# Per-edge coefficients of a graph network: three bf16 parts added in PSUM by TensorE, or in SBUF by VectorE

## The chip, the cores and the metric

One NeuronCore of a Trainium2 chip runs the whole kernel as one program. The metric is the device time of one execution in microseconds; a kernel's time is the median of its runs. Five engines work beside one another, each with its own instruction stream: TensorE (PE in the profile, its weight loads PEld), VectorE (DVE), ScalarE (ACT), GpSimd (POOL) and SyncE (SP), which issues DMAs. They meet by semaphores alone.

## The reference

A graph with 3125 nodes, 50000 edges sorted by destination, 128 features. Two blocks, each on the layer-normalised and rectified features, each added to its input:

```
def block_0(x, src, dst, W_in, b_in, W_out, b_out):
    h = x @ W_in + b_in                       # 64 wide
    ew = deg_inv_sqrt[src] * deg_inv_sqrt[dst]
    acc = cur = h
    for _ in range(3):
        cur = segment_sum(cur[dst] * ew, src)
        acc = acc + cur
    return acc / 4 @ W_out + b_out
def block_1(x, weight, w_comp, h_bias, loop_weight, norm, src, dst, etypes):
    W_rel = einsum('rb,bio->rio', w_comp, weight)      # 64 types, 16 bases
    msg = einsum('ni,rio->nro', x, W_rel)[src, etypes] * norm
    return relu(segment_sum(msg, dst) + h_bias + x @ loop_weight)
```

What the change touches is a part of block 1 that is done early: for each edge the 16 coefficients w_comp[type of the edge, :] times the weight `norm` of the edge. The edges lie in 391 tiles of 128.

## The kernel before, in words

**Setup** (to about 52 us). Edge data is loaded and tables of tiles and windows are made. A window is 16 destination nodes, 200 in all; a pair is a tile with one of the windows that it touches, S = 590 in all, worked through in 59 turns of U = 10.

**The counting stage** (about 52 to 345 us) makes the matrix CT of edge counts between nodes. Per turn VectorE (`onehots`, line 740) makes one-hot rows: every five pairs one L751, and for each pair one L754. They lie in a ring of three half turns; L749 waits until the pairs of the half that is overwritten are counted. TensorE (`count_pairs`, line 979) multiplies them, one matmul of 400 columns a pair (L992), into six rotating PSUM banks; it waits for VectorE's rows and for free banks in four groups a turn (pairs 0-2, 3-4, 5-7, 8-9). ScalarE copies two finished windows at a time out of PSUM (L1215) and clears them (L1217), SyncE stores them into CT (L426).

**The coefficients** ride along in the first 49 turns (CT_TURNS), 8 tiles of edges a turn. GpSimd loads the types of the edges, broadcast over partitions, into one of three buffers `cbuf` (`load_types`, L518), waiting for the coefficient matmuls that read the buffer before (`reload_types`, L522). After pair 4 VectorE turns them into a one-hot by type in place (`type_rows`, L721). After pair 6 TensorE multiplies them (L1000): four matmuls, each for two tiles, with 128x128 one-hot weights and a moving operand `wc_parts`. To have f32 accuracy from bf16 matmuls, w_comp is cut into three bf16 parts that add up to it (`finish_h`, L705 to L708), and the parts stand next to one another, so that the result has 2 x 16 x 3 = 96 columns. It goes to PSUM bank 6, which has no other use in these turns. In VectorE's next turn, after pair 7, a reduce adds the three parts from PSUM into `coef_sum` in SBUF (`sum_parts`, L727), and after pair 9 a multiply by the edges' weight makes `coef_out` (`finish_coefs`, L735), one of three buffers, which GpSimd stores to HBM (`store_coefs`, L529). TensorE may write bank 6 again when the reduce has read it (L996). L736 is the multiply's source.

The loops of three turns on the engines start at aligned instruction addresses. From turn 49 on there are no coefficients, and after each turn TensorE adds the columns of two finished groups of CT for the degrees (`add_degrees`, L1017, one-column matmuls, 25 a group).

**After it**: three rounds of propagation with CT (L1067, to about 520 us), the second layer norm, and block 1, which gathers rows by `src`, forms key rows with the stored coefficients (L873, L876), and multiplies (L1135, L1115). Nothing there is changed.

## Time and profile before

| | |
|---|---|
| Median of 3 runs | 1063.05 us (1062.24 to 1063.17) |
| The profiled execution | 1060.07 us |
| its span, first to last instruction | 1058.5 us |
| Mean granted TensorE clock | 0.886 |
| Busy: TensorE / VectorE / ScalarE / GpSimd | 835.4 / 777.0 / 357.5 / 477.5 us |
| Chain that ended last, by engine | TensorE 35%, VectorE 26%, issue 15% |

The span is what the trace covers; the execution's own time adds the little that lies before and after it. Busy shares are averages over stages with different limits, so a stage is read by itself. The granted clock is TensorE's share of full speed; it has two levels, 0.5 (1.2 GHz) and 1.0 (2.4 GHz). The record of an instruction lasts longer than it holds its engine up, as the next one starts before its end.

### The profile page before, as it was taken

The numbers are of one execution on the slowest core, as the hardware profiler recorded it, in microseconds if no ns is written. First come the engines' busy times: TensorE is split into PE (matmuls) and PEld (weight loads), VectorE is DVE, ScalarE is ACT, GpSimd is POOL, SyncE is SP. The second block draws the span as 40 slices with busy tenths as digits, with TensorE's granted clock in tenths as the row PEclk, the third lists the DMA queues.
The fourth block names the chain that finished last, engine by engine and source line by source line (L and its number), as shares of the span: only waits on it lengthen the run. The fifth ranks groups of instructions, "written<-read, shape, count | busy, mean of one in ns | idle before, by whom it ended". The sixth has DMA issues, their size and how long they took to land.

```text
span 1058.5 us, 27160 instructions
## 1 busy us (share of the span) xinstructions
PE 835.4 (79%) x5567; PEld 594.8 (56%) x5571; DVE 777.0 (73%) x2436; ACT 357.5 (34%) x706; POOL 477.5 (45%) x532
## 2 busy tenths in 40 slices
PE   4667667677698699999719889988888988888676
PEld 2622222222255699999517667666665665565345
DVE  7879999999984645434617777787778788888554
ACT  0402355677777000001315444443434332221000
POOL 2022323333200000010167777777777777777773
PEclk9687886977866899999858999999999999999868
DMA  4012334455534000011591111111112112111113
GB/s 114 1 45 67 85 103 107 125 131 128 132 101 107 2 1 2 1 32 51 146 298 49 48 50 50 50 50 47 52 47 52 50 50 52 50 52 51 51 50 89
DMA packets 64847, 73.24 MB, mean 69 GB/s; under 512 B 12803, under 2 KB 53178, under 8 KB 64666
## 3 DMA queue, kind: packets, MB, share of 16 engines
q1 hardware_dynamic: 48362, 37.30, 12.7%
q0 software_dynamic: 16432, 35.29, 12.6%
q8 instruction: 26, 0.43, 0.2%
q14 instruction: 27, 0.22, 0.1%
HBM read 43.85 MB, written 8.22 MB: 49 GB/s over the span
## 4 chain that ended last, share of the span: by engine, by line
PE 35%; DVE 26%; issue 15%; DVEq 9%; DMA 7%; POOL 5%; ACT 1%; SPq 1%; POOLq 0%; ACTq 0%
PE ps L1067 14%; PE ps L1135 10%; DMA CT<-h_dram,src_col 6%; POOL CT L563 5%; DVE ohbuf L754 5%; DVE CT L873 5%; PE ps L992 4%; PE ps L1115 3%; DVE u L754 3%; DVEq L876 3%; DVE CT L876 3%; DVE ohbuf L751 3%; DVEq L122 2%; DVEq L873 2%; DVE u L751 1%
## 5 line engine op out<-in xcount | busy, mean ns | idle before, releaser
L563 POOL DMA_INDIRECT CT<-h_dram,src_col x391 | 393.9, 1007 | 125.1 <-issue 95.4
L1135 PE MATMUL ps<-CT 128*128 128x256 f32 x1180 | 316.9, 418 | 71.7 <-DVE CT L876 46.3
L1135 PEld LDWEIGHTS ps<-CT 128*128 128x128 f32 x1180 | 211.3, 198 | 171.7 <-issue 151.9
L876 DVE SCALAR_TENSOR_TENSOR CT<-iota,dlP,CT 128x256 f32<-128x256 int16 x590 | 286.8, 486 | 5.6
L873 DVE COPY CT<-CT 128x128 f32 x590 | 137.7, 233 | 139.2 <-PE ps L1135 72.6
L1276 ACT COPY CT<-ps 128x256 f32<-128x256 f32 x200 | 77.7, 388 | 328.5 <-PE ps L1135 324.6
L992 PE MATMUL ps<-ohbuf 128*128 128x400 bf16 x395 | 126.6, 422 | 48.2 <-DVE ohbuf L754 34.6
L518 POOL DMA_DIRECT2D u<-types_dram x49 | 44.0, 904 | 198.8 <-PE ps L1000 185.1
L1215 ACT CAST stage<-ps 128x800 bf16<-128x800 f32 x100 | 82.4, 824 | 123.1 <-PE ps L992 122.8
L1067 PE MATMUL ps<-u,CT 128*128 128x192 bf16 x1250 | 107.4, 248 | 6.9 <-DVEq L804 6.9
L1067 PEld LDWEIGHTS ps<-u,CT 128*128 128x128 bf16 x1250 | 104.3, 99 | 9.0 <-DVEq L804 8.3
L992 PEld LDWEIGHTS ps<-ohbuf 128*128 128x128 bf16 x395 | 40.4, 102 | 122.6 <-issue 98.4
L754 DVE TENSOR_SCALAR ohbuf<-iota,keys 128x400 bf16<-128x400 int16 x395 | 102.4, 319 | 0.0
L1115 PE MATMUL ps<-CT 128*128 x800 | 95.8, 277 | 7.0 <-ACT CT L1276 4.8
L1115 PEld LDWEIGHTS ps<-CT 128*128 128x128 f32 x800 | 91.2, 191 | 16.9 <-issue 16.9
L992 PE MATMUL ps<-u 128*128 128x400 bf16 x195 | 64.3, 432 | 29.3 <-DVE u L754 17.2
L1217 ACT COPY ps<-zeros 128x800 f32<-128x800 f32 x100 | 83.0, 830 | 8.7
L551 POOL TENSOR_TENSOR ohbuf<-ohbuf,keys 128x640 f32<-128x640 f32 (+2 forms) x6 | 7.8, 1310 | 155.6 <-DMA ohbuf<-x 155.6
L1279 ACT COPY ps<-zeros 128x256 f32<-128x256 f32 x200 | 75.2, 376 | 6.5
L751 DVE TENSOR_TENSOR ohbuf<-iota,keys 128x640 bf16<-128x640 int16 x79 | 64.7, 819 | 9.5 <-PE ps L992 6.5
L1236 ACT ACTIVATE keys<-ps 128x256 f32<-128x256 f32 (+1 forms) x6 | 2.2, 366 | 161.5 <-PE ps L1041 161.5
L837 DVE COPY stage<-ps 128x320 f32<-128x320 f32 (+2 forms) x18 | 7.9, 436 | 66.2 <-PE ps L1067 65.7
(171 smaller groups left out, 653.9 us busy)
## 6 DMA issues: line engine op xcount, KB each, us to landing
CT<-stage SPq DMA_DIRECT2D x200, 100.0 KB, 3.0
u<-types_dram POOLq DMA_DIRECT2D x49, 128.0 KB, 3.5
CT<-h_dram,src_col POOLq DMA_INDIRECT x391, 2.6
coef_dram<-coef_out POOLq DMA_DIRECT2D x49, 64.0 KB, 3.4
CT<-coef_dram SPq DMA_DIRECT2D x1, 3048.0 KB, 11.9
out<-CT SPq DMA_DIRECT2D x4, 256.0 KB
ohbuf<-x SPq DMA_DIRECT2D x3, 320.0 KB, 3.8
x_dram<-ohbuf SPq DMA_DIRECT2D x3, 320.0 KB, 2.4
```

The lines of the kernel that those rows point to most:

```text
L563: pool.indirect_dma_start(out=gring[:, (j + 1) % GRING, :], out_offset=None, in_=h2_dram, in_offset=bass.IndirectOffsetOnAxis(ap=src_col[: ...
L751: dve.tensor_tensor(ohA[h][:], iota16[:, 0:P].unsqueeze(1).broadcast_to([P, HU, P]), keyP[:, cols].unsqueeze(2).broadcast_to([P, HU, P]), ...
L754: dve.tensor_scalar(ohB[h][:, u % HU, :], iota16[:], loP[:, col], None, ALU.is_equal).then_inc(oh_ready, 1)
L873: dve.tensor_copy(gpair[:, u:u + 1, :], gring[:, ds(pairs.place(total, GRING), 1), :]).then_inc(pair_in, 1)
L876: dve.scalar_tensor_tensor(kpair[:, u, :, :], iota_w, dl, coef_flat[:, ds(tiles * -BASES + NT * BASES, BASES)].unsqueeze(2) .broadcast_to( ...
L992: pe.matmul(bank_of(count_words[at], u - lo), ohA[h][:, u % HU, :], ohB[h][:, u % HU, :], start=False, stop=True, skip_group_check=True).t ...
L1067: ins = pe.matmul(psf[:, at:at + PART], CT[:, k, m * P:(m + 1) * P], u[:, k, :], start=(k == 0), stop=(k == NG - 1))
L1115: pe.matmul(bank, wrel[:, b, :], rows, start=(b == 0), stop=False)
L1135: pe.matmul(ps[:, ds(summed.place(counts[u][0], RING), 1), 0:WIN * BASES], gpair[:, u, :], kpair[:, u, :, :].rearrange("p b d -> p (b d)") ...
L1215: act.copy(stage[:, 2 * i:2 * i + 2, :], ps[:, bank:bank + 2, 0:LO]).then_inc(staged, 1)
L1217: act.copy(ps[:, bank:bank + 2, 0:LO], zeros[:].unsqueeze(1).broadcast_to([P, 2, LO])).then_inc(slots_free, 2)
L1276: act.copy(zsb[:, half, :, j * WIN:(j + 1) * WIN], ps[:, bank, 0:WIN * BASES].rearrange("p (b d) -> p b d", b=BASES)).then_inc(zcopied, 1)
```

## The change

The three parts are kept apart in `wc_parts`, each with its 2 x 16 columns contiguous. For each two tiles TensorE makes three matmuls of 32 columns, with the same weights, that add up in the same 32 columns of PSUM bank 6. The reduce, its buffer `coef_sum` and its semaphore `coef_read` are gone; the multiply reads PSUM, waits for the coefficient matmuls itself, and TensorE waits for the multiply (`coef_cp`) before it writes the bank again.

```diff
--- before.py
+++ after.py
@@ -74,7 +74,7 @@
 FIELDS = 5
 CCH = 8
 COEF_MM = 6
-COEF_TYPES, COEF_SUM, COEF_OUT = 4, 7, 9
+COEF_TYPES, COEF_OUT = 4, 9
 CHALF = CCH * P // 2
 PARTS = 3
 HALVES = 3
@@ -188,9 +188,8 @@
         typ = sb("typ", [P, 1], F32)
         norm_col = sb("norm_col", [P, NT + 1], F32)
         wc_sb = sb("wc_sb", [P, 2, BASES], F32)
-        wc_parts = sb("wc_parts", [P, 2, BASES, PARTS], BF16)
+        wc_parts = sb("wc_parts", [P, PARTS, 2, BASES], BF16)
         wc_rest = sb("wc_rest", [P, 2, BASES], F32)
-        coef_sum = sb("coef_sum", [P, CCH * BASES], F32)
         coef_out = sb("coef_out", [P, HALVES, CCH * BASES], F32)
 
 
@@ -341,7 +340,6 @@
         et_in = [sem(f"et_in{b}") for b in range(HALVES)]
         typed = sem("typed")
         coef_mm = sem("coef_mm")
-        coef_read = sem("coef_read")
         coef_cp = sem("coef_cp")
         coef_st = [sem(f"coef_st{b}") for b in range(HALVES)]
         passed = sem("passed")
@@ -702,10 +700,10 @@
             def finish_h():
 
                 dve.wait_ge(ld_par, 64)
-                step(dve.tensor_copy(wc_parts[:, :, :, 0], wc_sb[:]))
-                step(dve.tensor_tensor(wc_rest[:], wc_sb[:], wc_parts[:, :, :, 0], ALU.subtract))
-                step(dve.tensor_copy(wc_parts[:, :, :, 1], wc_rest[:]))
-                step(dve.tensor_tensor(wc_parts[:, :, :, 2], wc_rest[:], wc_parts[:, :, :, 1], ALU.subtract))
+                step(dve.tensor_copy(wc_parts[:, 0], wc_sb[:]))
+                step(dve.tensor_tensor(wc_rest[:], wc_sb[:], wc_parts[:, 0], ALU.subtract))
+                step(dve.tensor_copy(wc_parts[:, 1], wc_rest[:]))
+                step(dve.tensor_tensor(wc_parts[:, 2], wc_rest[:], wc_parts[:, 1], ALU.subtract))
                 dve.wait_ge(hmul, H_TURNS)
                 for bank in range(4, 8):
                     lo = 8 * (bank - 4)
@@ -720,20 +718,13 @@
                 dve.wait_ge(et_in[b], loaded)
                 dve.tensor_scalar(cbuf[:, b, :], cbuf[:, b, :], typ[:, 0:1], None, ALU.is_equal).then_inc(typed, 1)
 
-            def sum_parts(c):
+            def finish_coefs(c, b, stored):
                 dve.wait_ge(coef_mm, c + 1)
-                if not (isinstance(c, int) and c == 0):
-                    dve.wait_ge(coef_cp, c)
-                dve.tensor_reduce(coef_sum[:], ps[:, COEF_BANK, 0:CCH * BASES * PARTS].rearrange("p (n k) -> p n k", k=PARTS),
-                                  AX.X, ALU.add).then_inc(coef_read, 1)
-
-            def finish_coefs(c, b, stored):
-                dve.wait_ge(coef_read, c + 1)
                 if stored is not None:
                     dve.wait_ge(coef_st[b], stored)
                 tiles = slice(c * CCH, (c + 1) * CCH) if isinstance(c, int) else ds(c * CCH, CCH)
                 dve.tensor_tensor(coef_out[:, b].rearrange("p (h i b) -> p i h b", h=2, b=BASES),
-                                  coef_sum[:].rearrange("p (i h b) -> p i h b", h=2, b=BASES),
+                                  ps[:, COEF_BANK, 0:CCH * BASES].rearrange("p (i h b) -> p i h b", h=2, b=BASES),
                                   norm_col[:, tiles].rearrange("p (h i) -> p i h", h=2).unsqueeze(3)
                                   .broadcast_to([P, CCH // 2, 2, BASES]), ALU.mult).then_inc(coef_cp, 1)
 
@@ -754,8 +745,6 @@
                     dve.tensor_scalar(ohB[h][:, u % HU, :], iota16[:], loP[:, col], None, ALU.is_equal).then_inc(oh_ready, 1)
                     if u == COEF_TYPES and loaded is not None:
                         type_rows(c, phase, loaded)
-                    if u == COEF_SUM and coefs:
-                        sum_parts(c - 1)
                     if u == COEF_OUT and coefs:
                         finish_coefs(c - 1, (phase - 1) % HALVES, stored)
 
@@ -993,12 +982,14 @@
                               stop=True, skip_group_check=True).then_inc(pairs_done, 1)
                     if coefs and u == COEF_MM:
                         if not (isinstance(c, int) and c == 0):
-                            pe.wait_ge(coef_read, c)
+                            pe.wait_ge(coef_cp, c)
                         pe.wait_ge(typed, c + 1)
                         for i in range(CCH // 2):
-                            n = 2 * BASES * PARTS
-                            last = pe.matmul(ps[:, COEF_BANK, i * n:(i + 1) * n], cbuf[:, phase, i * P:(i + 1) * P],
-                                             wc_parts[:].rearrange("p h b k -> p (h b k)"), start=True, stop=True)
+                            n = 2 * BASES
+                            for k in range(PARTS):
+                                last = pe.matmul(ps[:, COEF_BANK, i * n:(i + 1) * n], cbuf[:, phase, i * P:(i + 1) * P],
+                                                 wc_parts[:, k].rearrange("p h b -> p (h b)"), start=(k == 0),
+                                                 stop=(k == PARTS - 1))
                         last.then_inc(coef_mm, 1)
 
             count_pairs(0, 0)
```

## Rows read from the trace of the kernel before

**Rows 1.** Windows: us; busy us (count) of PE, PEld, DVE, ACT, POOL; clock; DMA
```profile
81.00:277.00 196.00, 136.32 (x574) 54.66 (x574) 195.96 (x617) 110.08 (x134) 62.24 (x82) 0.78 0.42 110
277.00:292.00 15.00, 10.54 (x46) 4.35 (x47) 14.78 (x49) 12.38 (x16) 1.64 (x4) 0.84 0.45 117
292.00:330.00 38.00, 34.66 (x478) 19.55 (x477) 32.80 (x102) 29.63 (x37) 0.52 (x1) 0.72 0.40 104
```

**Rows 2.** Waits of 81 to 292 us: total us, times, longest
```profile
PE ps L992 <- DVE ohbuf L754: 30.1, 45, 1.1
PE ps L992 <- DVE u L754: 16.1, 20, 1.1
DVE ohbuf L751 <- PE ps L992: 0.2, 1, 0.2
```

**Rows 3.** Timeline of VectorE in one turn (start us, us)
```profile
152.35 0.54 DVE L727 TENSOR_REDUCE coef_sum<-ps 128x128 f32<-128x384 f32 x1
152.82 0.54 DVE L754 TENSOR_SCALAR u<-iota,keys 128x400 bf16<-128x400 int16 x2
153.29 0.28 DVE L735 TENSOR_TENSOR coef_out<-coef_sum,norm_col 128x128 f32<-128x128 f32 x1
153.49 0.81 DVE L751 TENSOR_TENSOR ohbuf<-iota,keys 128x640 bf16<-128x640 int16 x1
```

**Rows 4.** Single lines (ns min/median/max, first and last start); VectorE's stall at its loop
```profile
L727 DVE TENSOR_REDUCE coef_sum<-ps x49: 541/549/564, 58.8 to 290.5; 128x128 f32<-128x384 f32 x49
...
L1000 PEld LDWEIGHTS ps<-wc_parts,u x196: 95/105/152, 57.2 to 287.0; 128*128 128x128 bf16 x196
L1000 PE MATMUL ps<-wc_parts,u x196: 206/281/288, 57.3 to 287.1; 128*128 128x96 bf16 x196
...
77.05 0.83 DVE L751 TENSOR_TENSOR ohbuf<-iota,keys 128x640 bf16<-128x640 int16 x1 [2.85 <-issue]
```

**Rows 5.** Last of the four setup lines that the change touches
```profile
L708 DVE TENSOR_TENSOR wc_parts<-wc_rest,wc_parts x1: 214/214/214, 49.9 to 49.9; 128x32 bf16<-128x32 f32 x1
```

**Rows 6.** VectorE groups of 345 to 545 us, from PSUM and from SBUF
```profile
L838 DVE TENSOR_TENSOR stage<-ps,stage 128x128 f32<-128x128 f32 x3 | 0.9, 291 | 0.1
...
L801 DVE TENSOR_TENSOR stage<-stage,u 128x128 f32<-128x128 f32 x2 | 0.6, 293 | 0.1
```

**Rows 7.** Timeline of TensorE in the turn of rows 3
```profile
152.86 0.56 PE L992 MATMUL ps<-u 128*128 128x400 bf16 x2 [0.69 <-DVE u L754]
153.25 0.33 PE L1000 MATMUL ps<-wc_parts,u 128*128 128x96 bf16 x4
...
153.95 0.56 PE L992 MATMUL ps<-u 128*128 128x400 bf16 x2 [0.20 <-ACT ps L1217]
155.43 0.79 PE L992 MATMUL ps<-ohbuf 128*128 128x400 bf16 x3 [0.92 <-DVE ohbuf L754]
```

**Rows 8.** One-column matmuls: the window, and the timeline in it
```profile
297.30:298.90 1.60, 1.57 (x51) 1.43 (x49) 1.60 (x6) 1.51 (x2) 0.00 (x0) 0.50 0.49 130
...
297.35 1.52 PE L1017 MATMUL ps<-ones_bf,CT 128*128 128x1 bf16 x50
```

**Rows 9.** Windows at the high and low clock; timeline of TensorE at the low
```profile
105.00:109.80 4.80, 2.78 (x14) 1.16 (x14) 4.80 (x16) 1.66 (x2) 1.11 (x2) 1.00 0.42 108
162.60:167.40 4.80, 3.75 (x15) 1.29 (x15) 4.80 (x16) 2.70 (x4) 1.11 (x2) 0.52 0.39 89
167.40:172.20 4.80, 4.08 (x16) 1.57 (x15) 4.80 (x17) 2.83 (x4) 1.71 (x2) 0.50 0.44 120
...
167.80 0.53 PE L1000 MATMUL ps<-wc_parts,u 128*128 128x96 bf16 x4
...
169.72 1.85 PE L992 MATMUL ps<-ohbuf 128*128 128x400 bf16 x5 [0.40 <-DVE ohbuf L754]
```

**Rows 10.** DMA issues of 215 to 292 us (KB each, median us to landing)
```profile
u<-types_dram POOLq DMA_DIRECT2D x13, 128.0 KB, 3.9
```

**Rows 11.** Timeline of TensorE in the propagation: eleven matmuls in a row
```profile
359.83 1.07 PE L1067 MATMUL ps<-u,CT 128*128 128x192 bf16 x11
```

## The prediction, made blind

> **What bounds the kernel now.** I read the windows first, to see which engine fills which stretch [rows 1]. From 81 to 277 us VectorE is busy 195.96 of 196.00 us, TensorE 136.3, ScalarE 110.1. From 292 us on TensorE is the fullest (34.66 of 38.00). Second, the waits of 81 to 292 us [rows 2]: VectorE waits once, for 0.2 us, while TensorE waits 30.1 + 16.1 = 46.2 us for one-hot rows of VectorE. So the coefficient stage is set by VectorE's instruction stream, and every instruction in it has its full price. Third, one turn of the timeline [rows 3]. A turn of ten pairs holds two L751, ten L754, L721, the reduce L727 and the multiply L735.
>
> On VectorE the records overlap by their fixed ends, so I price by the distance from start to start. The reduce starts at 152.35 and the next L754 at 152.82: 0.47 us, though the record says 0.54. The multiply takes from 153.29 to the next L751 at 153.49: 0.20 us [rows 3]. The 49 reduces start from 58.8 to 290.5 us; less one stall of 2.85 us on entering VectorE's loop [rows 4], a turn is (231.7 - 2.85) / 48 = 4.77 us.
>
> **The change, part by part.**
> Setup: the four instructions at L705 to L708 stay four, with a contiguous side where a stride was. One takes 0.21 us at 32 elements [rows 5], nearly all of it fixed. 0, at most 0.1 us either way.
>
> The reduce goes: 49 x 0.47 = 23.0 us of VectorE. The last one, in turn 49, stands at 290.5 us, where TensorE takes over as the bound, so 48 count: **-22.6 us**. Its waits go too; VectorE never waits there, so they are worth nothing.
>
> The multiply reads PSUM where it read SBUF. The trace has a pair for this: a 128x128 f32 operation on two tensors takes 291 ns with one of them in PSUM (L838) and 293 with both in SBUF (L801) [rows 6]. So +0. The bounds: no gain, since the reduce, which reads PSUM too, shows (549 - 280) / 256 = 1.05 ns an element more than the multiply and thus the same fixed part [rows 3, 4]; as a loss one more fixed part, 0.20 us less 128 x 1.05 ns = 0.07 us a turn, 3.4 us in all.
> The Trainium skill (VectorE: DVE Perf Modes, the section on the TRN2 errata) speaks against the change here: a fixed part of 58 cycles for SBUF sources and 120 for PSUM, at 0.96 GHz. As an estimate from that page it is 65 ns a turn, 3.1 us of the gain, and a time of 1044. The rows above show no such difference, and the rows decide.
>
> The multiply now waits for the coefficient matmuls of the turn before. TensorE issues those at 153.25 us [rows 7], as VectorE ends that turn, and VectorE asks at the end of the next: over 3 us early. 0. What is queued behind it are the next turn's one-hots, for which TensorE waits.
>
> TensorE's new wait is the one to look at. Before the coefficient matmuls of turn c it waited for the reduce, after pair 7 of VectorE's turn; now for the multiply, after pair 9. Without the reduce the one-hots of pairs 8 and 9 start at 152.35 and 152.59 and the multiply at 152.82, with its record ended at 153.10 [rows 3]; TensorE comes to the coefficient matmuls at 153.25 [rows 7]. The wait is met with 0.15 us to spare, or costs up to 0.2 us if the signal is slow. Behind it stand the matmuls of pairs 7 to 9 and then those of the next turn, which now stand idle 0.92 us for VectorE [rows 7]. So 0; if that cover went, 0.2 x 48 = 10 us.
>
> Twelve matmuls of 32 columns for four of 96: the same 384 columns. The nearest rows for a short matmul with its own weight load are L1017's, one column each: 50 in 1.52 us at the low clock (granted 0.50) [rows 8], 30 ns each. 32 columns take 13 ns at 2.4 GHz and 27 at 1.2 GHz, so I take 30 ns: 0.36 us for the twelve. Four of 96 columns cost (0.33 - 0.21) / 3 = 40 ns each at the high clock [rows 4, 7] and (0.53 - 0.28) / 3 = 83 at the low one [rows 4, 9]: 0.16 and 0.33 us. So +0.20 us of TensorE a turn at the high clock, +0.03 at the low. Upper bound: 83 ns for each of the twelve, 1.0 us, +0.8 and +0.7. Lower: no cost.
>
> Has TensorE room for a turn of 4.77 - 0.47 = 4.30 us? At the high clock yes: 2.78 busy of 4.80 [rows 9]. The low clock (1.2 GHz) holds about 44% of the time, as the mean is 0.78 [rows 1]. There TensorE is busy 4.08 of 4.80, and still waits 0.40 us for VectorE before a turn [rows 9]: its own turn is 4.77 - 0.40 = 4.37 us, changed 4.40. That is 0.10 over VectorE's new turn. VectorE feels it only when its lead is used up. It starts a turn (153.49) once the pairs of the turn before the last are done, and that was at 153.95 + 0.56 - 4.77 = 149.74 [rows 3, 7]: a lead of 3.7 us, 3.2 in shorter turns. The low stretch from about 162.6 to 172.2 us lasts two turns [rows 9], a lag of 0.2 us. 0.
>
> ScalarE's copies: late windows are denser, and from 277 to 292 us it is busy 12.38 of 15.00 [rows 1], 3.94 us a turn, 92% of 4.30. It just fits; for the last turns I book +0.6 us. GpSimd's type loads land 3.9 us after their issue [rows 10]; they are issued after the coefficients of turn c and used in turn c + 3, over 8 us later. 0. The queues of SP and GpSimd issue what they did.
>
> **What comes after** shifts rigidly: from turn 49 on TensorE sets the pace with the degree columns.
>
> Sum: -22.6 + 0.6 = **-22.0 us**, against the profiled execution's own 1060.07 us (span 1058.5): 1038.1. The runs shown have their median 3.0 us above that execution, so for the median 1063.05 - 22.0 = **1041.0 us**.
>
> **The rivals.**
> A. TensorE or ScalarE takes over as the bound. For it: 4.40 us at the low clock against 4.30, and ScalarE at 92% late on. Against: the low clock holds 44% of the time, and the lead is over 3 us. Were the clock low throughout and TensorE's turn 4.45 with the new wait, the gain would be (4.77 - 4.45) x 48 = 15 us: 1048. Chance 0.10.
> B. The weight loads show. Each of the twelve matmuls loads 128x128 weights again, and such a load has a record of 105 ns [rows 4]; uncovered, the twelve cost 1.26 us, 0.93 more than now at the low clock and 1.1 at the high one. TensorE's turn is then 4.37 + 0.93 = 5.3 us at the low clock. There 21 turns lose 0.53 us, 11 us, and the other 27 gain 0.47, 13 us; with VectorE's lead evening out a little, 1057 to 1063, about 1060. Against: L1017 does just this, load and one column, in 30 ns [rows 8]. Chance 0.03, a third of it faster by more than 0.2%.
> The Trainium skill (TensorE: Matmul & The Clock Gate, on LDWEIGHTS) has a rule by which B would hold: columns / 1.2 ns for a load, an estimate of 107 ns here. L1017's spacing does not agree with it as a cost.
> C. Slower: the three matmuls into one PSUM range wait for one another, each for its whole record. The shortest record of 96 columns is 206 ns [rows 4], with 32 columns about 0.18 us, twelve 2.2 us. TensorE's turn would be 4.37 + 2.2 - 0.33 = 6.2 us at the low clock. At the high one, 2.78 busy [rows 9] and about 0.6 of gaps between groups, 3.4 + 2.2 - 0.16 = 5.4. The mean of 5.8 is 1.0 more than now: 1063 + 48 = 1111 us. It decides from 0.33 + 0.40 = 0.73 us for the twelve at the low clock (61 ns each). Against it: the propagation adds 25 matmuls of 192 columns into one range, eleven in 1.07 us [rows 11], under 100 ns each. Chance 0.03.
> D. The reduce did not bind: VectorE's saved time goes to a wait that the trace counts as busy, or to more stalls like the one of 2.85 us. The records are contiguous, and that stall comes once. Within 0.2% (2 us, about what a measurement of this kernel can tell from no change). Chance 0.02.
>
> **How the numbers follow.** The forecast keeps 0.82, with its own range of 1038 to 1045: down by 0.6 and 2 us of scatter and shifted stalls, up by the 3.4 us of the PSUM bound. With A, 0.10 at about 1048, the range is 1037.5 to 1048.5; B, C, D and the outer part of A stay outside. Faster by over 0.2%: the forecast, A and a third of B, 0.93; within it the rest of B and D, 0.04; slower C, 0.03.
>
> **What the changed profile would show.** L727 gone; L735 still near 285 ns; VectorE full, in turns of 4.30 us; 588 L1000 matmuls some 30 ns apart; TensorE's wait for VectorE at L1000 under 0.2 us a turn; the coefficient stage ending near 270 in place of 292 us, and later stages as long as before. The size is wrong if TensorE's waits for VectorE vanish (A), the sign if L751 waits for TensorE in most turns (C).

## The result, and the profile after

The changed kernel takes **1035.58 us** (median of 4 runs, 1033.22 to 1036.52), the kernel before, run beside it, 1062.64 us (4 runs, 1060.84 to 1063.17): a ratio of 0.9745, 95% interval 0.9725 to 0.9765. It is faster by 27.1 us where 22.0 were forecast. The profiled execution took 1033.22 us, its span 1031.7, with a mean granted clock of 0.916 (before 0.886).

First the windows of the changed kernel (columns as in [rows 1]: span of the window, busy time and count of PE, PEld, DVE, ACT, POOL, then clock, DMA share, GB/s).

```profile
81.00:277.00 196.00, 145.64 (x1122) 64.44 (x1123) 196.00 (x642) 130.13 (x160) 60.19 (x84) 0.90 0.50 125
...
81.00:250.00 169.00, 123.84 (x877) 53.24 (x876) 169.00 (x557) 107.09 (x132) 57.31 (x79) 0.90 0.50 124
250.00:270.00 20.00, 15.15 (x134) 7.12 (x135) 20.00 (x66) 16.88 (x22) 2.88 (x6) 0.94 0.52 132
270.00:310.00 40.00, 36.62 (x482) 20.10 (x480) 29.56 (x92) 32.63 (x42) 0.00 (x0) 0.71 0.40 105
```

VectorE is full up to 270 us, as it was up to 292 [rows 1]; the stage in which TensorE sets the pace follows from there. TensorE's granted clock in the coefficient stage rose from 0.78 to 0.90.

Now the instructions of two lines (engine, operation, count: shortest/median/longest ns, first to last start). L726 is the multiply, which was L735; L990 are the coefficient matmuls, which were L1000.

```profile
L726 DVE TENSOR_TENSOR coef_out<-ps,norm_col x49: 274/280/300, 58.4 to 264.4; 128x128 f32<-128x128 f32 x49
...
L990 PE MATMUL ps<-wc_parts,u x588: 176/176/234, 56.6 to 261.3; 128*128 128x32 bf16 x196
```

The multiply reads PSUM and has a median of 280 ns; from SBUF it had 283. The reduce is gone. Next the timeline of VectorE in one turn, the counterpart of [rows 3] (start, duration, engine, line).

```profile
149.50 0.28 DVE L726 TENSOR_TENSOR coef_out<-ps,norm_col 128x128 f32<-128x128 f32 x1
149.70 0.81 DVE L742 TENSOR_TENSOR ohbuf<-iota,keys 128x640 bf16<-128x640 int16 x1
150.43 1.25 DVE L745 TENSOR_SCALAR ohbuf<-iota,keys 128x400 bf16<-128x400 int16 x5
151.60 0.34 DVE L719 TENSOR_SCALAR u<-u,typ 128x512 bf16<-128x512 bf16 x1
151.86 0.81 DVE L742 TENSOR_TENSOR u<-iota,keys 128x640 bf16<-128x640 int16 x1
152.59 1.24 DVE L745 TENSOR_SCALAR u<-iota,keys 128x400 bf16<-128x400 int16 x5
153.76 0.28 DVE L726 TENSOR_TENSOR coef_out<-ps,norm_col 128x128 f32<-128x128 f32 x1
```

From multiply to multiply it is 4.26 us, and from the multiply to the next one-hot 0.20 us, the same as from SBUF [rows 3]. TensorE at the same time, the counterpart of [rows 7]:

```profile
153.84 0.56 PE L981 MATMUL ps<-u 128*128 128x400 bf16 x2 [0.20 <-DVE u L745]
154.23 0.45 PE L990 MATMUL ps<-wc_parts,u 128*128 128x32 bf16 x12
```

Twelve matmuls with their weight loads take 0.45 us where four took 0.33. One record is 176 ns, so it is (0.45 - 0.18) / 11 = 25 ns from one to the next. The waits of 57 to 270 us (total, times, longest) hold just one row for L990 and none that names VectorE:

```profile
PE ps L981 <- DVE ohbuf L745: 19.3, 60, 1.2
PE ps L981 <- DVE u L745: 15.0, 30, 1.3
...
DVE ohbuf L742 <- PE ps L981: 4.0, 2, 2.5
...
PEld ps L990 <- issue: 1.5, 8, 0.2
```

**Where the 27 us came from.** The start-to-start distance of the 49 multiplies gives every turn's length, and it falls into three kinds. A pass of VectorE's hardware loop is three turns long, and there are 14 passes. So 13 turns begin with the jump back to the loop's head, and turn 5 begins with the entry into the loop.

| | before | after | difference |
|---|---|---|---|
| normal turn | 4.730 | 4.265 | 0.465 |
| the 13 turns with a jump back | 4.88 | 4.265 | 0.465 + 0.15 |
| the turn with the loop entry | 7.66 | 5.83 | 0.465 + 1.37 |
| first to last multiply | 231.7 | 206.0 | 25.7 |

48 x 0.465 = 22.3, 13 x 0.15 = 2.0 and 1.4 make the 25.7. Ahead of the first multiply lie one more reduce (0.47) and 0.9 us of setup and first matmuls, in which the two executions differ. The whole is 27.0, and the end of the degree columns moves by just that, from 346.16 to 319.19 us. From the first matmul of the propagation, at 349.96 and 322.99 us, the rest takes 708.5 and 708.7 us.

So 22.8 us are the reduce. The 2.0 and the 1.4 us are something else, and they are the question of the experiments. The stall at the loop entry was 2.85 us [rows 4]; in the changed kernel's timeline it stands as

```profile
71.17 0.27 DVE L726 TENSOR_TENSOR coef_out<-ps,norm_col 128x128 f32<-128x128 f32 x1
72.92 0.82 DVE L742 TENSOR_TENSOR ohbuf<-iota,keys 128x640 bf16<-128x640 int16 x1 [1.48 <-PE ps L981]
```

The sequencer (DVEq in the profile) is the part of VectorE that reads the program and hands instructions on. Its records tell what happened at the entry. The line that puts the loop at an aligned address (L767 before, L756 after) is a branch, and the first record of the loop line comes about 3 us behind it. First the kernel before, then the changed one:

```profile
L767 DVEq COMPARE_BRANCH  x1: 53/53/53, 73.6 to 73.6; - x1
L770 DVEq MOVE  x1: 36/36/36, 76.7 to 76.7; - x1
...
L756 DVEq COMPARE_BRANCH  x1: 53/53/53, 69.8 to 69.8; - x1
L759 DVEq MOVE  x1: 36/36/36, 72.6 to 72.6; - x1
```

The last instruction ahead of the loop, the multiply, starts at 73.92 and 71.17 us. So the branch was 0.3 us ahead of it before, and 1.35 us after: that much more of the 3 us is hidden.

And this is VectorE at a jump back in the kernel before:

```profile
161.81 0.55 DVE L727 TENSOR_REDUCE coef_sum<-ps 128x128 f32<-128x384 f32 x1
162.28 0.55 DVE L754 TENSOR_SCALAR ohbuf<-iota,keys 128x400 bf16<-128x400 int16 x2
162.74 0.29 DVE L735 TENSOR_TENSOR coef_out<-coef_sum,norm_col 128x128 f32<-128x128 f32 x1
163.03 0.82 DVE L751 TENSOR_TENSOR ohbuf<-iota,keys 128x640 bf16<-128x640 int16 x1
```

From multiply to one-hot it is 0.29 us here, against 0.20 in a turn without the jump [rows 3]. What the sequencer did then, from the records of the loop line L770 and the multiply's line:

```profile
L735 DVEq FUSED_REGOPS  x1: 57/57/57, 162.4 to 162.4; - x1
...
L770 DVEq COMPARE_BRANCH  x1: 56/56/56, 162.6 to 162.6; - x1
```

The sequencer computes the multiply's addresses at 162.4 us, right as the reduce ends (161.81 + 0.55 = 162.36), and jumps at 162.6, 0.14 us before the multiply starts. It is held by the wait for coef_read, which VectorE's own reduce sets, with two one-hots, 0.47 us together, between reduce and multiply. In the changed kernel the same instruction stands at

```profile
L759 DVEq COMPARE_BRANCH  x1: 56/56/56, 146.6 to 146.6; - x1
```

and the multiply of that turn runs at 149.50: the sequencer is 2.9 us ahead.

### The profile page after: what moved, and what is told of

It reads as the page before. It is cut to its first block, busy times and chain, and to the rows that moved or that the text cites. A ratio compares the mean times of both kernels' runs of the same rounds, so it can differ in the third digit from the quotient of the medians.

```text
span 1031.7 us, 27847 instructions
## 1 busy us (share of the span) xinstructions
PE 824.9 (80%) x5959; PEld 594.5 (58%) x5963; DVE 752.2 (73%) x2387; ACT 356.9 (35%) x706; POOL 474.3 (46%) x532
## 4 chain that ended last, share of the span: by engine, by line
PE 35%; DVE 25%; issue 15%; DVEq 9%; DMA 8%; POOL 5%; ACT 2%; SPq 1%; POOLq 0%; ACTq 0%
PE ps L1058 14%; PE ps L1126 13%; DVE ohbuf L745 7%; DMA CT<-h_dram,src_col 7%; POOL CT L561 5%; DVE CT L862 5%; DVE u L745 3%; PE ps L981 3%; PE ps L1106 3%; DVE CT L865 3%; DVEq L865 2%; DVEq L122 2%; DVEq L745 2%; DVEq L862 2%; DVE ohbuf L742 1%
## 5 line engine op out<-in xcount | busy, mean ns | idle before, releaser
L1126 PEld LDWEIGHTS ps<-CT 128*128 128x128 f32 x1180 | 208.0, 196 | 173.4 <-issue 155.2
L981 PE MATMUL ps<-ohbuf 128*128 128x400 bf16 x395 | 120.5, 392 | 33.6 <-DVE ohbuf L745 14.6
L516 POOL DMA_DIRECT2D u<-types_dram x49 | 35.8, 735 | 176.3 <-PE ps L990 162.8
L1106 PEld LDWEIGHTS ps<-CT 128*128 128x128 f32 x800 | 91.2, 191 | 16.9 <-issue 16.9
L745 DVE TENSOR_SCALAR ohbuf<-iota,keys 128x400 bf16<-128x400 int16 x395 | 99.0, 318 | 0.0
L981 PE MATMUL ps<-u 128*128 128x400 bf16 x195 | 58.2, 378 | 26.9 <-DVE u L745 12.3
## 6 DMA issues: line engine op xcount, KB each, us to landing
CT<-coef_dram SPq DMA_DIRECT2D x1, 3048.0 KB, 12.7
```

The lines of the kernel that those rows point to most:

```text
L745: dve.tensor_scalar(ohB[h][:, u % HU, :], iota16[:], loP[:, col], None, ALU.is_equal).then_inc(oh_ready, 1)
L981: pe.matmul(bank_of(count_words[at], u - lo), ohA[h][:, u % HU, :], ohB[h][:, u % HU, :], start=False, stop=True, skip_group_check=True).t ...
L1106: pe.matmul(bank, wrel[:, b, :], rows, start=(b == 0), stop=False)
L1126: pe.matmul(ps[:, ds(summed.place(counts[u][0], RING), 1), 0:WIN * BASES], gpair[:, u, :], kpair[:, u, :, :].rearrange("p b d -> p (b d)") ...
```

## The experiments

**Theory S** (the sequencer): a wait of VectorE for its own recent result keeps its sequencer from running ahead. With the jump only 0.14 us ahead of the multiply it shows as 0.15 us, and the loop entry shows nearly in full; the change took the wait away along with the reduce. **Rivals**: L, that the loop body is shorter, or lies elsewhere, so that its jump costs less; P, that the multiply from PSUM costs more, and more than the reduce's price came back elsewhere; T, that TensorE's twelve matmuls, or its higher clock, gave something by themselves.

**The changed kernel again.** It ran on each of three more chips, to show how far a whole run can be trusted. The runs with the wait for pair 8, the reduce after pair 5, TensorE's half and the types on GpSimd ran on a fourth, beside the kernel before alone; where they are compared with the changed kernel, it is across chips.

> The changed kernel once more, as the measure for the others on this chip. Theory S (VectorE's sequencer: in the kernel before, the multiply waited for the reduce two instructions ahead of it, so the sequencer could not run ahead of the engine and each loop branch showed): 27 us under the kernel before, of which 22.9 from the 49 reduces, 2.0 from 13 loop branches and 1.4 from the stall on entering the loop; VectorE's turns are 4.26 us throughout. Rival N (scatter): the gain falls back towards 23 us, and the setup's 0.8 us goes with it.

1035.24 us (5 runs, 1034.14 to 1036.03), before 1060.39 (15 runs), ratio 0.976 [0.9745, 0.9775]. The turns are those of the first profile: 4.265, 4.266 with a jump, 6.00 at the entry, 206.2 us in all. The gain of 25.2 us is close to the 25.5 of the stage (231.7 - 206.2); the further 1.3 us ahead of it did not show, as the first multiply starts at 59.90 us here and at 59.71 in the kernel before. Over all the profiles the first one-hot starts between 44.3 and 46.0 us.

> The changed kernel a third time, as the measure for the run beside it and for the scatter between chips and profiles: 1034 to 1037 us, turns of 4.26 to 4.27 us, stall at the loop's start 1.5 to 1.8 us.

1035.18 us (4 runs), before 1062.1 (7), ratio 0.9751 [0.9719, 0.9784]; turns 4.265, entry 5.82, stage 206.1.

> The changed kernel beside it on the same chip: 1034 to 1037 us.

1036.37 us (5 runs), before 1060.27 (9), ratio 0.978 [0.9761, 0.9799]; turns 4.265, entry 6.07, stage 206.3. The stage repeats within 0.3 us and the time within 1.2, while the gain over the kernel before is 25.2, 26.9 and 23.9 us beside the first 27.1. So theories about 1 to 3 us are read from the stage.

**The wait alone, put back.** In the changed kernel the multiply also waits for VectorE's own one-hot of pair 7, so that two one-hots (pairs 8 and 9) lie between, as between reduce and multiply in the kernel before. A turn counts U + 2 = 12 one-hot instructions, and pair 7 is the tenth of them.

```
             def finish_coefs(c, b, stored):
+                dve.wait_ge(oh_ready, c * (U + 2) + (U + 2 + 8 + 2))
                 dve.wait_ge(coef_mm, c + 1)
```

> The changed kernel with a wait of VectorE for its own one-hot of pair 7 ahead of the multiply, where the kernel before waited for the reduce; no work added. Theory S: every third turn is 0.15 us longer again and the stall at the loop's start 1.4 us, +3.4 us over the changed kernel. Rival L (the five us of gain beyond the reduces came from shorter code or its place): no change, 0 +- 1 us.

1039.66 us (5 runs, 1035.28 to 1039.87), ratio 0.9795 [0.9774, 0.9816]. Normal turns stay at 4.265, the 13 with a jump are 4.36 (+0.10) and the one with the entry is 6.88 (+0.8 to 1.05). Its stall in the timeline:

```profile
70.68 0.28 DVE L727 TENSOR_TENSOR coef_out<-ps,norm_col 128x128 f32<-128x128 f32 x1
73.48 0.82 DVE L743 TENSOR_TENSOR ohbuf<-iota,keys 128x640 bf16<-128x640 int16 x1 [2.52 <-PE ps L982]
```

The stage is 208.4 us, 2.2 more than in the changed kernel beside it. A wait of VectorE for itself, which adds no work, costs 2.2 us, and it does so only at the jumps and the entry. That is the way S says, but less than its 3.4: the jumps cost 0.10 and not 0.15 us, the entry about 0.9 and not 1.4.

**The wait one pair later**, for pair 8, so that one one-hot is left between. The code is as long as in the experiment above.

```
-                dve.wait_ge(oh_ready, c * (U + 2) + (U + 2 + 8 + 2))
+                dve.wait_ge(oh_ready, c * (U + 2) + (U + 2 + 9 + 2))
```

> The changed kernel with VectorE's wait ahead of the multiply for its own one-hot of pair 8 in place of pair 7, 0.235 us later. Theory S gives a dose: the turns with a branch go from 4.36 to about 4.59 us, 13 x 0.235 = 3.1 us more than with pair 7, the stall at the loop's start another 0.2 us, together about 3.3 us over the run with pair 7 and 5.5 over the changed kernel; the other turns stay 4.27 as long as the sequencer still needs less than one one-hot for the multiply. Rival L: as the run with pair 7, since the code has the same length.

1043.9 us (4 runs, 1041.68 to 1045.79), ratio 0.9851 [0.9831, 0.9871]. Turns with a jump are 4.69 (+0.32 on the last kernel), the others 4.30 (+0.04, which S did not forecast), the entry 7.30, and the stage 214.1, 5.8 more where 3.3 were expected. The timeline now shows the jump as a stall, with nothing that it waited for:

```profile
96.10 0.28 DVE L727 TENSOR_TENSOR coef_out<-ps,norm_col 128x128 f32<-128x128 f32 x1
96.33 0.82 DVE L743 TENSOR_TENSOR u<-iota,keys 128x640 bf16<-128x640 int16 x1
...
100.41 0.28 DVE L727 TENSOR_TENSOR coef_out<-ps,norm_col 128x128 f32<-128x128 f32 x1
100.92 0.82 DVE L743 TENSOR_TENSOR ohbuf<-iota,keys 128x640 bf16<-128x640 int16 x1 [0.24 <-issue]
```

The price follows the place of the wait while the code stays as long: L falls. The size of the dose is above what S forecast.

**The reduce earlier, in the kernel before**, after pair 5 and then after pair 1 where it stood after pair 7. The work is the same; only the distance from VectorE's reduce to the multiply that waits for it grows, to four one-hots and then to ten instructions (eight L754, L721 and L751).

```
-COEF_TYPES, COEF_SUM, COEF_OUT = 4, 7, 9
+COEF_TYPES, COEF_SUM, COEF_OUT = 4, 5, 9
```

> The kernel before with its reduce after pair 5 of the turn in place of pair 7, two one-hots further from the multiply. Theory S (VectorE's sequencer waits for the reduce to end before it can place the multiply and reach the branch; 0.15 us of the branch showed): the 13 long turns of 4.87 us go, the stall at the loop's start shrinks by about 0.5 us as two one-hots more lie ahead; the coefficient stage is 2.0 + 0.5 = 2.5 us shorter than the 231.7 us of before, and as the reduce waits for nothing in turn 1 (after pair 1 it waited for TensorE), all of it arrives: 2.5 us under the kernel before. Rival L (code length or place): no change.

1058.82 us (12 runs, 1057.25 to 1060.31), before 1060.03 (29 runs), ratio 0.9983 [0.9973, 0.9993]. Normal turns 4.733, turns with a jump 4.735: the 0.15 us is gone. The entry turn is 6.85 (before 7.66), the stage 229.1, 2.6 less than before, where 2.5 were expected. The time is 1.2 us less, with 0.7 to 2.9 as its interval. The stall:

```profile
74.03 0.28 DVE L735 TENSOR_TENSOR coef_out<-coef_sum,norm_col 128x128 f32<-128x128 f32 x1
76.34 0.83 DVE L751 TENSOR_TENSOR ohbuf<-iota,keys 128x640 bf16<-128x640 int16 x1 [2.04 <-PE ps L992]
```

> The kernel before with its reduce after pair 1 of the turn in place of pair 7; the multiply stays after pair 9. All work and all waits stay, only the multiply's wait for the reduce is met long before. Theory S: 3.4 us under the kernel before, turns of 4.73 us without exception, stall at the loop's start about 1.5 us. Rival L: no change, 0 +- 1 us. If TensorE's later wait for the multiply mattered in the changed kernel, nothing of it shows here, as TensorE's wait is only met sooner.

1059.43 us (11 runs), before 1060.39, ratio 0.9988 [0.9977, 1.0]. The turns with a jump are 4.733, the same as the others, and the entry turn is 5.22, 2.4 shorter. The stage is 227.5, 4.2 less. The time is only 1.0 us less (0.0 to 2.4). Part of the reason is in the trace: in the first turn VectorE now waits for TensorE,

```profile
57.77 0.56 DVE L727 TENSOR_REDUCE coef_sum<-ps 128x128 f32<-128x384 f32 x1 [4.17 <-PE ps L1000]
```

so that the first multiply comes 1.5 us later (61.24 for 59.71). That leaves 2.7 us. From the first matmul of the propagation the rest took 710.9 us here and 711.0 in the run with the reduce after pair 5, and between 708.5 and 710.7 in all other profiles; with one trace each, whether that is scatter or belongs to the edit stays open. In the stage, two one-line edits of the old kernel thus give what S says, with nothing changed on TensorE.

**What the sequencer waits for, in every trace.** The branch ahead of the loop shows it best, since it comes once. In each of the 14 profiles it stands 0.04 to 0.05 us behind the end of what the multiply waits for. Six of them:

| run | ends (us) | branch | ahead of the last instruction | stall, start to start |
|---|---|---|---|---|
| wait for pair 8 | one-hot, 71.03 | 71.07 | 0.11 | 3.14 |
| kernel before | reduce, 73.54 | 73.58 | 0.34 | 3.12 |
| wait for pair 7 | one-hot, 70.30 | 70.34 | 0.34 | 2.81 |
| reduce after pair 5 | reduce, 73.17 | 73.22 | 0.81 | 2.31 |
| changed kernel | TensorE's L990, 69.77 | 69.82 | 1.35 | 1.75 |
| reduce after pair 1 | reduce, 72.66 | 72.71 | 2.74 | 0.67 |

From the branch to the loop's first one-hot it is 3.1 to 3.5 us in each of the 14 profiles; the stall is that, less the lead. So the stall that the changed kernel keeps has the same cause: its multiply waits for coef_mm, and at the entry TensorE's coefficient matmuls end only 1.4 us before the multiply starts. Inside the loop they end over 3 us before it, and the sequencer is 2.9 us ahead.

The 2.8 to 3.2 us from the branch to the loop's first record go with a transfer of instructions. The DMA view of the changed kernel for 69.7 to 72.7 us has this row (packets, MB, share):

```profile
q14 instruction: 1, 0.01, 0.8%
```

It is one packet of 8 KB, and in each of the 14 profiles such a packet starts 1.0 to 1.1 us behind this branch and takes 0.3 to 0.95 us. VectorE has two more branches to an aligned loop (L766 and L872 in the changed kernel). There no such packet comes between, and the loop's first record is 0.53 us behind the branch in every profile. So at the first loop the sequencer most likely waits for the loop's code; no experiment moved the code to test it.

**Does the multiply pay for PSUM?** In the changed kernel a copy of 128 columns from PSUM to SBUF comes after pair 1, and the multiply reads the copy (TensorE then waits for the copy, not the multiply).

```
+            def copy_coefs(c):
+                dve.wait_ge(coef_mm, c + 1)
...
+                dve.tensor_copy(coef_sum[:], ps[:, COEF_BANK, 0:CCH * BASES]).then_inc(coef_read, 1)
...
-                dve.wait_ge(coef_mm, c + 1)
+                dve.wait_ge(coef_read, c + 1)
...
-                                  ps[:, COEF_BANK, 0:CCH * BASES].rearrange("p (i h b) -> p i h b", h=2, b=BASES),
+                                  coef_sum[:].rearrange("p (i h b) -> p i h b", h=2, b=BASES),
```

> The changed kernel with the sum in PSUM copied to SBUF after pair 1 (128 columns) and the multiply reading SBUF. TensorE waits for the copy, not for the multiply. If the PSUM source costs nothing (forecast): +0.20 us a turn for the copy, 49 x 0.20 = 9.8 us over the changed kernel, and the multiply's record stays at 0.28 us. If a PSUM source costs 0.07 us more: +6.4 us. If TensorE's wait for the multiply cost time in the changed kernel, it comes off here too.

1047.96 us (4 runs, 1046.54 to 1048.7), ratio 0.9881 [0.9863, 0.9899]: 12.7 us over the changed kernel, of which the stage has 10.5 (216.7 us). The groups of lines, 57 to 292 us (total busy us, mean ns):

```profile
L727 DVE COPY coef_sum<-ps 128x128 f32<-128x128 f32 x49 | 13.7, 280 | 4.2 <-PE ps L1000 4.1
L734 DVE TENSOR_TENSOR coef_out<-coef_sum,norm_col 128x128 f32<-128x128 f32 x49 | 13.7, 280 | 0.0
```

The same multiply has 280 ns from SBUF too. Had reading PSUM cost 0.07 us, the multiply would have given that back and a turn had grown by 0.20 - 0.07 = 0.13 us; it grew by 0.25 on average (4.513 for 4.265). The turns come in two lengths, 4.47 and 4.53 us. The shorter is the copy's 0.20 us and no more; in the longer ones a one-hot two behind the copy has a record of 0.38 us in place of 0.31. P falls. What stretches that one-hot is not shown. The entry turn, 4.94 us, is 1.1 shorter than in the changed kernel, as the copy after pair 1 takes over the wait for coef_mm.

**TensorE's half alone.** In the kernel before, the four matmuls of 96 columns become twelve of 32 that don't accumulate; each part has its own range, and the reduce still adds them, with a stride.

```
-                            n = 2 * BASES * PARTS
-                            last = pe.matmul(ps[:, COEF_BANK, i * n:(i + 1) * n], cbuf[:, phase, i * P:(i + 1) * P],
-                                             wc_parts[:].rearrange("p h b k -> p (h b k)"), start=True, stop=True)
+                            n = 2 * BASES
+                            for k in range(PARTS):
+                                at = k * CCH * BASES + i * n
+                                last = pe.matmul(ps[:, COEF_BANK, at:at + n], cbuf[:, phase, i * P:(i + 1) * P],
+                                                 wc_parts[:, k].rearrange("p h b -> p (h b)"), start=True, stop=True)
```

> TensorE's part of the change alone, on the kernel before: twelve matmuls of 32 columns for four of 96, without accumulation (the parts lie 128 columns apart in the bank) and the reduce adds them with a stride of 128 elements. Forecast: VectorE-bound as before, no change, 0 +- 1 us, the twelve matmuls 0.36 us + one record, and L992 not later for VectorE. If the strided reduce costs VectorE more, its record exceeds 0.55 us and its distance to the next one-hot 0.47 us. If more matmuls cost (the low-clock rival): slower by up to 10 us. What the clock does: the granted mean in 81 to 250 us, 0.78 before and 0.90 to 0.93 in the changed kernel, stays near 0.78 if it rose for the shorter turns, and is near 0.9 if it rose for the twelve matmuls.

1060.46 us (12 runs), before 1060.03, ratio 1.0006 [0.9992, 1.002]. The turns are 4.745, with a jump 4.85, the entry 7.57, the stage 231.6. From 81 to 250 us:

```profile
81.00:250.00 169.00, 119.22 (x777) 49.47 (x773) 168.97 (x532) 90.62 (x110) 51.04 (x72) 0.78 0.41 106
```

The clock stays at 0.78. TensorE's half costs nothing and gives nothing: T falls, and the clock of 0.90 came with the shorter turns. The adding up in one range of PSUM is not part of this run.

**The multiply earlier**, after pair 5. Here TensorE's new wait for it would be met long before.

```
-COEF_TYPES, COEF_OUT = 4, 9
+COEF_TYPES, COEF_OUT = 4, 5
```

> The changed kernel with its multiply after pair 5 of VectorE's turn in place of pair 9, so that TensorE's wait for it before the coefficient matmuls is met about 0.9 us sooner; nothing else. By the forecast that wait was met with 0.15 us to spare or hidden behind TensorE's idle time: no change, 0 +- 1 us, turns of 4.27 us, and no waits of TensorE's L990 in either. Rival: the wait had a price inside TensorE's turn (up to 0.2 us, 10 us in all) that VectorE's full records hide: faster by more than 2 us, or a shorter stall at the loop's start. A stall shorter than the 1.6 to 1.7 us of the changed kernel would say that the place of the multiply and its wait still holds VectorE's sequencer back.

1035.71 us (5 runs), before 1060.27, ratio 0.9763 [0.975, 0.9777]; the changed kernel beside it has 1036.37. Turns 4.265, entry 5.79, stage 206.0. Neither kernel shows a wait of L990 for VectorE, so the wait placed after pair 9 costs nothing. The stall at the loop entry doesn't depend on the multiply's place either: TensorE's coefficient matmuls end at 70.95 us here and the branch stands at 71.00, so it is the same wait for coef_mm.

**A faster VectorE still.** In the changed kernel the type one-hot works on 16 of its 512 columns and the multiply on 8 of 128. So the kernel leaves out the coefficients (`coef_out` is set to zero once in the setup); all waits and transfers stay.

```
-                dve.tensor_scalar(cbuf[:, b, :], cbuf[:, b, :], typ[:, 0:1], None, ALU.is_equal).then_inc(typed, 1)
+                dve.tensor_scalar(cbuf[:, b, 0:16], cbuf[:, b, 0:16], typ[:, 0:1], None, ALU.is_equal).then_inc(typed, 1)
...
+                dve.tensor_tensor(coef_out[:, b, 0:CCH], ps[:, COEF_BANK, 0:CCH],
+                                  norm_col[:, tiles], ALU.mult).then_inc(coef_cp, 1)
```

> How much further VectorE can be unloaded before another engine binds: the changed kernel with the types' one-hot made for 16 of 512 columns and the multiply for 8 of 128, so the coefficients are not computed; all instructions, waits and transfers stay. By (512 - 16) / 4 = 124 cycles of 1.04 ns and 120 of 1.04 ns VectorE's turn falls by 0.13 + 0.125 = 0.25 us to 4.01 us, if both ran at the rates seen. If VectorE stays the bound: 49 x 0.25 = 12.5 us under the changed kernel. By the forecast's count ScalarE needs 3.94 us a turn late in the stage and TensorE 4.40 at the low clock; if they bind, turns of irregular length appear late in the stage, VectorE waits for TensorE at the start of half turns, and 3 to 5 us of it don't arrive.

1036.36 us (4 runs, 1035.05 to 1037.98), ratio 0.9765 [0.9731, 0.98], against 0.9751 [0.9719, 0.9784] for the changed kernel beside it: no gain, where some 8 us were expected. The turns are 4.01 us up to about the fourteenth, and 4.25 on average after that, (259.50 - 114.95) / 34. The window of 81 to 250 us and a wait in it, which the changed kernel has not (there VectorE waits twice, 4.0 us in all, both before 81 us):

```profile
81.00:250.00 169.00, 122.96 (x878) 53.31 (x879) 163.50 (x563) 106.37 (x130) 48.35 (x80) 0.92 0.49 124
...
DVE u L741 <- PE ps L980: 4.3, 9, 0.7
```

VectorE is idle 5.5 us of the window. The stage is 203.2 us, 2.9 less than in the changed kernel beside it, and even that does not last: TensorE's degree columns end at 320.9 us in both. So TensorE, with ScalarE's copies behind it, does a turn in about 4.25 us. The changed kernel's 4.265 lies on that: it has used up the room, and less work for VectorE alone gives nothing more. Whether TensorE or ScalarE sets the 4.25 was not separated.

**A version that moves the type one-hot to GpSimd**, to beat both.

```
+            def type_rows(c, b, loaded):
+                pool.wait_ge(et_in[b], loaded)
...
+                pool.tensor_scalar(cbuf[:, b, :], cbuf[:, b, :], typ[:, 0:1], None, ALU.is_equal).then_inc(typed, 1)
...
-                    if u == COEF_TYPES and loaded is not None:
-                        type_rows(c, phase, loaded)
```

> A candidate: the changed kernel with the types' one-hot (0.26 us of VectorE a turn) made by GpSimd, which waits most of this stage. If VectorE remains the bound: turns of 4.00 us, 49 x 0.26 = 12.7 us under the changed kernel, 1022. ScalarE then has 3.94 us a turn to do late in the stage and TensorE's low-clock turn is 4.40, so about 4 us less than that: 1026. Rival: GpSimd's operation takes over 3 us or slows VectorE's one-hots (their record grows over 0.32 us), and the time rises above the changed kernel's.

1057.52 us (12 runs), ratio 0.9976 [0.9965, 0.9986], 22 us slower than the changed kernel. The groups of 81 to 277 us and a piece of the timeline:

```profile
L527 POOL TENSOR_SCALAR u<-u,typ 128x512 bf16<-128x512 bf16 x42 | 77.0, 1834 | 0.9 <-DMA u<-types_dram 0.6
L750 DVE TENSOR_TENSOR ohbuf<-iota,keys 128x640 bf16<-128x640 int16 x55 | 55.2, 1004 | 0.0
```

```profile
152.66 1.62 POOL L527 TENSOR_SCALAR u<-u,typ 128x512 bf16<-128x512 bf16 x1
152.67 1.41 DVE L750 TENSOR_TENSOR ohbuf<-iota,keys 128x640 bf16<-128x640 int16 x1
...
155.47 0.81 DVE L750 TENSOR_TENSOR u<-iota,keys 128x640 bf16<-128x640 int16 x1
```

VectorE saves one instruction of 0.26 us a turn and pays more: its one-hot takes 1.41 us beside GpSimd's operation and 0.81 without it, and a turn has 4.77 us. This version is slower than the changed kernel.

## Why the prediction was right, and where it was wrong

**The mechanism held.** VectorE's instruction stream set the stage, and the 49 reduces came off at their start-to-start price: 0.465 us measured, 0.47 used. VectorE stayed full, the stage ended near 270 us, the rest of the kernel kept its length.

**The multiply from PSUM at +0** was right: 280 ns and 0.20 us to the next start, from either memory, in the change and in the copy experiment. The Trainium skill (VectorE: DVE Perf Modes, the section on the TRN2 errata) has a fixed part 62 cycles longer for PSUM; as an estimate from that page the time would have been 3.1 us longer, and neither kernel shows that. The row [rows 6] was the better guide.

**Twelve matmuls at 30 ns** measured 25 at the high clock and (0.53 - 0.23) / 11 = 27 at the low one (twelve in 0.53 us from 74.11 us on, granted clock 0.50). Rivals B and C are out with it: the twelve take 0.45 us, where B had 1.26 and C 2.2.

**TensorE's new wait at 0** was right, and the experiment with the multiply after pair 5 shows that the price is none. The multiply's record ends at 154.04 us and TensorE comes to its matmuls at 154.23, so the room was 0.19 us where 0.15 was forecast.

**The step that failed** is this one: "Its waits go too; VectorE never waits there, so they are worth nothing." The waits never showed as VectorE's idle time, but they held its sequencer. Removing the wait for coef_read was worth 13 x 0.15 = 2.0 us at the jumps and 1.4 us at the loop entry (1.1 to 1.4 over the four profiles of the changed kernel). The prediction put these at nothing. It took the mean turn of 4.77 as the turn, when it was 4.730 and sometimes 4.88, and treated the stall of 2.85 us as fixed ("that stall comes once"). The experiments show the link from both sides: such a wait put into the changed kernel costs 2.2 us of stage, and one pair later 8.0 us, and in the old kernel a reduce two pairs earlier gives 2.6. The size was not forecast well from either side (3.4 and 5.5 us were expected for the first two), but the sequencer's records name the mechanism.

**Smaller errors** make up the rest. The 0.6 us booked for ScalarE did not come: from 250 to 270 us it is busy 16.88 of 20.00, 84%, and VectorE is full. One reduce more counts (49 x 0.465 = 22.8 for 22.6). And 0.9 us ahead of the first coefficients is the scatter of the setup, luck on the side of the gain: on the other chips the whole was 23.9 to 26.9 us. Together 2.0 + 1.4 + 0.6 + 0.2 + 0.9 = 5.1 us, which is the distance from 22.0 to 27.0 but for rounding. The start counted too: the prediction went from a median of 1063.05 us, and the kernel before had 1060.0 to 1062.1 on the other chips, so that all four medians of the changed kernel, 1035.2 to 1036.4, lie under the range's 1037.5. The range's lower end allowed 2 us for "scatter and shifted stalls", and 3.4 us of stalls went.

**Rival A** did not happen, but was closer than its chance says. The changed turn of 4.265 us lies at the 4.25 that TensorE and ScalarE allow. It did not bind for a reason that the prediction did not have: it took the low clock as holding 44% of the time, while the clock rose to 0.90 as the turns grew shorter.

**Open**: whether the loop's entry loses its 3 us when its code is fetched ahead; why the wait for pair 7 costs 0.10 us at a jump where the wait for the reduce costs 0.15, and why the other turns grow by 0.04 with the wait for pair 8; and which of TensorE and ScalarE limits a turn to 4.25 us.

## What to carry to other kernels

Price a removed wait by what it holds, not by the idle time in front of it: an engine's wait for its own recent result keeps its sequencer close behind it, and then the jumps of a loop and the loop entry show. Look for turns of unequal length, since a mean turn hides them, and read the sequencer's records at the loop line. Here a jump back was free with four one-hots between VectorE's result and its own wait for it; the entry would need some 3 us of work behind the last wait ahead of it. Before the next reduction of the fullest engine, run one with part of its work left out: it shows how much room is left.

## What the runs showed of the hardware

- A wait of VectorE for its own one-hot with two one-hots between cost nothing in normal turns and 0.10 us in the 13 with a jump; with one between it cost 0.04 and 0.42 us (4.30 and 4.69 for 4.265). In the old kernel the wait for the reduce cost 0.15 us at a jump with two one-hots between, and 0.00 with four or more.
- VectorE's branch into its loop stood 0.04 to 0.05 us behind the end of what the multiply, the last instruction with a wait ahead of it, waits for, in all 14 profiles; from the branch to the loop's first one-hot it was 3.1 to 3.5 us. To the loop's first record it was 2.8 to 3.2 us with an 8 KB packet of the instruction queue in between, and 0.53 us without one, at its two later loops.
- TensorE's granted clock from 81 to 250 us went with the length of the turns, at nearly equal work in each: 0.77 to 0.78 at 4.73 to 4.78 us (0.81 with the types on GpSimd), 0.85 at 4.51, 0.87 at 4.41 (the wait for pair 8), 0.90 to 0.94 at 4.265. Twelve short matmuls in place of four in turns of the old length left it at 0.78.
- A GpSimd operation on 128x512 bf16 (1.83 us on average) beside VectorE's 128x640 one-hot stretched that from 0.81 to 1.41 us.
- A load of 128x128 bf16 weights with a matmul of 32 columns went by in 25 ns, at the low clock in 27, though the load's record has a mean of 99.
